# Writing the mask of a windowed attention with four 64x64 products instead of two of 128x128

## The chip, the cores and the metric

One core of a Trainium2 chip runs the whole program. The metric is the device time in microseconds, the median of three runs. The program is written by hand: each engine (TensorE, VectorE, ScalarE, GpSimd and the SyncE DMA queue) has its own list of instructions in a fixed order, and the engines meet only at semaphores.

## What is computed

Two transformer layers, each with a conditioning vector that scales, shifts and gates its two halves. Only the attention of the first layer is touched. For 8 sequences of 512 tokens and width 128, with 16 heads of 64, it is, cut to what matters:

```python
H, D, window_size = (16, 64, 32)
xn = rms_norm(x)
q, k, v = jnp.split(xn @ w_qkv.T, 3, axis=-1)      # 16 heads of 64
q, k = apply_rope(q, cos, sin), apply_rope(k, cos, sin)
attn = jnp.einsum('bhqd,bhkd->bhqk', q, k) * scale
mask = (q_pos >= k_pos) & (q_pos - k_pos <= window_size)
attn = jax.nn.softmax(jnp.where(mask, attn, NEG), axis=-1)
out = jnp.einsum('bhqk,bhkd->bhqd', attn, v)        # then @ w_out.T
```

Each query sees itself and the 32 keys ahead of it. After it follow a router with experts, the second layer's attention and a feed-forward stage in emulated FP4; they stay as they are.

## The kernel before

`phase_attention0` goes through the 8 sequences. A sequence is cut into 16 units: unit `u` has a group of four heads, `q = u // 4`, and a tile of 128 tokens, `t = u % 4`. For a unit the scores are kept for 64 queries at a time: 64 queries see at most 96 keys (the 32 ahead of them and their own 64), so one head gives a block of 64 x 96, and four heads with two halves of the tile fill `psS[:, s]`: 128 partitions (half `a` of the tile on partitions 64a to 64a+63), two PSUM banks (`j`), and in a bank two blocks of 96 columns (`i`).

`score(b, u)` on TensorE fills these banks. First the mask is written: for each bank `j` one bf16 product of a 128x128 identity with 192 columns of the mask table (line 417), which sets the bank to 0 or -1e9. Then the eight fp32 products of queries and keys are added to it (line 425), each of 64x64 weights with 96 columns and thus on one quarter of the array: `j` chooses the rows, `a` the columns. An fp32 product is two instructions. The mask table has two halves of 192 columns: one for `t == 0`, where the first 64 queries of a sequence have no keys ahead of them, and one for the other three tiles.

The order of the work in the body of a unit `u` of sequence `b`:

- TensorE: four transposes of the unit's probabilities into `psT` (line 530), `score(b, u + 2)`, a piece of the projection of the head group after the next (`project`, lines 442 and 447), then, when ScalarE has copied the transposed probabilities, the products with the values into `psO` (line 550), and in units of `t` 2 and 3 a second piece of the projection. After the 16th unit comes the output projection (line 487), after the 8th the transposes of the next sequence's input. `PLAN` gives the pieces: piece 0 in units of t = 0, 1 in t = 1, 2 and 3 in t = 2, 4 and 5 in t = 3.
- VectorE: the division of the probabilities of unit u + 1 (lines 703 and 704), the sine product of one half of a later group (line 676), and the row maxima of unit u + 2 (line 670) together with the sum that ends the rotary embedding (`rope`, line 685). In units of t = 1 this sum stands ahead of the maxima, in the others behind them. `score` of t = 0 waits for this sum. The first units of a sequence also hold steps of the next sequence's normalisation (lines 301, 805 and 808, and line 319 for statistics).
- ScalarE: the copy of the last unit's output (line 626), the copy of the transposed probabilities (line 649, `probT`), the copy of a projected piece out of PSUM (line 589 or 594), the four exponentials of unit u + 2 (line 575).
- GpSimd: one cosine product (line 835, `qk_cos`) for every projected piece of queries or keys, as soon as ScalarE has copied it.
- SyncE: DMAs that swap the halves of a copied piece, and those that lay out the values.

So the score of unit u + 2 is made early: its maxima, exponentials, division and transposes follow in the next two units.

Of the kernel before, what the change touches and what calls it, by code (L numbers as in the profile page):

```python
# [24 lines left out]
HALF = P // 2  # L25
KW = WIN + HALF
# [30 lines left out]
def wait(engine, sem, value):  # L57

    if not (isinstance(value, int) and value <= 0):
        engine.wait_ge(sem, value)  # L60
# [261 lines left out]
def phase_attention0(nc, k):  # L322
# [5 lines left out]
    with ExitStack() as ctx:  # L328
# [13 lines left out]
        psS = ctx.enter_context(nc.psum_tensor("psS", [P, 2, 2, 512], F32))  # L342
# [66 lines left out]
        def _(pe):  # L409
            def score(b, u):  # L410

                q, t = u // TILES, u % TILES
                s, par = u % 2, q % 2
                if t == 0:
                    wait(pe, roped, b * HALVES * QUADS + HALVES * q + HALVES)
                for j in range(2):
                    nc.tensor.matmul(psS[:, s, j, 0:2 * KW], k.ident_bf[:, :], k.mask[:, (t == 0) * 2 * KW:((t == 0) + 1) * 2 * KW],
                                     start=True, stop=False, skip_group_check=True)
                for i in range(2):
                    for a in range(2):  # L420
                        lo = 0 if t == 0 and a == 0 else WIN
                        q0 = t * P + a * HALF
                        for j in range(2):
                            rows = slice(D * j, D * j + D)
                            last = nc.tensor.matmul(psS[a * HALF:(a + 1) * HALF, s, j, i * KW + WIN - lo:(i + 1) * KW],  # L425
                                                    qk[rows, par, i, 0, q0:q0 + HALF],
                                                    qk[rows, par, i, 1, q0 - lo:q0 + HALF],
                                                    start=False, stop=True, skip_group_check=True)
                last.then_inc(scored, 1)
# [54 lines left out]
            def out_project(b, pairs, first, last_):  # L484
# [5 lines left out]
                if last_:  # L490
# [8 lines left out]
                             start=True, stop=True).then_inc(w_turned, 1)  # L499
# [7 lines left out]
            for n in range(len(OPENING)):  # L507
                if OPENING[n] == (0, 1):
                    pe.wait_ge(w_dve, 1)
                if OPENING[n] == (0, 3):  # L510
                    pe.wait_ge(w_act, 2)
                    turn_sixth(4)
                    turn_sixth(5)
                opening(n)
                if OPENING[n] == (1, 1):
                    pe.wait_ge(w_dve, 3)
                    score(0, 0)
                    score(0, 1)
            pe.wait_ge(w_act, 5)

            def body(b, last):
                for u in range(UNITS):
# [9 lines left out]
                    if not (last and u + 2 >= UNITS):  # L532
                        score(b, u + 2)
# [1692 lines left out]
```

## Time and profile before

| | |
|---|---|
| time, median of 3 runs | 1284.41 us (1284.17 to 1285.26) |
| span of the profiled execution | 1295.1 us |
| first attention in it | from about 37 us to 600 us |
| one sequence of it in steady state | 68.6 us |
| PE busy in such a sequence | 62.5 us of 68.6 us |
| mean of a mask product (line 417) | 254 ns, x256 |

The profiled execution has no time of its own beside its span; it is 10.7 us (0.8%) over the median of the timed runs. In the rows, PE is a matmul on TensorE and PEld the load of its weights; a matmul's duration runs from its start to the end of its results, and the next one may start long before that. Rows of the timeline merge instructions of the same line, with their number behind "x".

### The profile page before, as it was taken

To read this page: it belongs to the slowest core of one execution; us is meant where nothing else is said; L and a number is where in the kernel's file an instruction comes from. 1 tells how busy PE (TensorE), PEld (TensorE's weight loads), DVE (VectorE), ACT (ScalarE), POOL (GpSimd) and SP (SyncE) were. 2 spreads that over 40 slices of the span, in tenths; PEclk is the share of its full clock that TensorE was granted. 3 is DMA by queue.
4 is the path that set the end of the run, shared out by engine and by line. 5 is a ranking of instruction groups with operands and counts; after the bars stand their busy time and mean duration, and the time that the engine had idled before them with its cause. 6 is when DMAs were issued, how large, how long until landed. Compare 5 with 4: busy or idle time off the path is not lost. (4 is left out here: it accounts for less than half of the span.)

```text
span 1295.1 us, 25137 instructions
## 1 busy us (share of the span) xinstructions
PE 975.8 (75%) x8604; PEld 662.5 (51%) x8604; DVE 805.3 (62%) x1683; ACT 639.2 (49%) x2132; POOL 430.4 (33%) x332
## 2 busy tenths in 40 slices
PE   6779998989899999985613769747348787867665
PEld 3456565656656565664503556534225454545454
DVE  5777758687777767564657514112136878559995
ACT  3565767767676767671101323112038777643322
POOL 2334333333342423321000857886611312200221
PEclk9789899999999998987555789888759999868967
DMA  6564343434443434431402123445310000000000
GB/s 198 150 182 107 92 123 88 119 96 113 102 113 100 113 83 107 104 91 42 102 0 62 45 59 69 61 73 129 31 66 1 1 2 1 1 1 9 17 17 25
DMA packets 89009, 93.62 MB, mean 72 GB/s; under 512 B 18800, under 2 KB 62304, under 8 KB 88944
## 3 DMA queue, kind: packets, MB, share of 16 engines
q1 hardware_dynamic: 78576, 84.12, 24.7%
q0 software_dynamic: 10368, 8.66, 4.7%
q8 instruction: 37, 0.61, 0.2%
q14 instruction: 28, 0.23, 0.1%
HBM read 24.36 MB, written 10.70 MB: 27 GB/s over the span
## 5 line engine op out<-in xcount | busy, mean ns | idle before, releaser
L835 POOL TENSOR_TENSOR qk_cos<-qk_raw,const 128x512 f32<-128x512 f32 x128 | 183.2, 1432 | 313.0 <-ACT qk_raw L589 313.0
L575 ACT ACTIVATE prob<-psS,neg_max 128x96 f32<-128x96 f32 x512 | 167.9, 342 | 86.5 <-DVE neg_max L670 85.7
L442 PE MATMUL psQ<-a_xnT,weights 128*128 128x512 f32 x250 | 146.0, 668 | 2.1 <-ACT a_xnT L621 1.4
L550 PEld LDWEIGHTS psO<-probT,v_windows 96*64 96x64 f32 x2048 | 73.7, 143 | 142.6 <-ACT probT L649 121.1
L550 PE MATMUL psO<-probT,v_windows 96*64 96x64 f32 x2048 | 91.8, 235 | 43.9 <-ACT probT L649 43.9
L685 DVE TENSOR_TENSOR qk_roped<-qk_cos,qk_swapped 128x512 f32<-128x512 f32 x128 | 119.0, 929 | 5.9 <-DVE qk_swapped L676 5.5
L1508 POOL DMA_INDIRECT sums<-ex_y,ex_index x64 | 97.6, 1525 | 39.5 <-issue 23.5
L1497 POOL DMA_INDIRECT ex_rows<-rows,ex_index x64 | 67.1, 1048 | 121.8 <-DMA ex_index<-lists 102.6
L575 ACT ACTIVATION_READ_ACCUMULATOR prob<-psS,neg_max 128x1 f32 x512 | 105.4, 206 | 0.0
L1442 ACT ACTIVATE ex_hidden<-ex_psH,ex_b 128x512 f32<-128x512 f32 x64 | 43.7, 687 | 114.4 <-PE ex_psH L1401 59.7
L649 ACT COPY probT<-psT 96x512 f32<-96x512 f32 x128 | 76.8, 600 | 46.5 <-PE psT L530 46.5
L589 ACT COPY qk_raw<-psQ 128x512 f32<-128x512 f32 x125 | 74.0, 592 | 48.0 <-PE psQ L442 44.7
L676 DVE TENSOR_TENSOR qk_swapped<-qk_swapped,const 128x512 f32<-128x512 f32 x128 | 88.8, 694 | 14.2 <-DMA qk_swapped<-qk_raw 14.2
L1401 PE MATMUL ex_psH<-ex_hT,ex_w 128*128 128x512 f32 x128 | 69.4, 683 | 18.6 <-ACT ex_hidden L1442 17.8
L530 PE MATMUL psT<-const,prob 128*96 128x128 f32 x512 | 82.3, 285 | 0.0
L703 DVE RECIPROCAL prob_rsum<-prob_sum 128x4 f32<-128x4 f32 x128 | 22.4, 175 | 93.0 <-ACT prob L575 92.9
L704 DVE TENSOR_TENSOR prob<-prob,prob_rsum 128x384 f32<-128x384 f32 x128 | 75.4, 589 | 4.4
L425 PE MATMUL psS<-qk_roped 64*64 64x96 f32 (+1 forms) x2048 | 74.4, 259 | 0.0
L447 PE MATMUL psQ<-weights,a_xnT 128*128 128x256 f32 x252 | 72.7, 412 | 0.0
L670 DVE TENSOR_REDUCE neg_max<-psS 128x4 f32<-128x384 f32 x128 | 70.5, 550 | 3.5 <-PE psS L425 3.5
L1410 PE MATMUL ex_psY<-ex_w,ex_hidden 128*128 128x128 f32 x512 | 64.5, 287 | 10.4 <-issue 10.4
L1410 PEld LDWEIGHTS ex_psY<-ex_w,ex_hidden 128*128 128x128 f32 x512 | 63.1, 203 | 11.6 <-issue 11.5
(317 smaller groups left out, 1936.2 us busy)
## 6 DMA issues: line engine op xcount, KB each, us to landing
qk_swapped<-qk_raw SPq DMA_DIRECT2D x512, 64.0 KB, 2.0
v_windows<-v_tok SPq DMA_DIRECT2D x32, 384.0 KB, 4.4
v_windows<-v_tok SPq DMA_DIRECT2D x32, 256.0 KB, 3.6
mod<-mod_rows SPq DMA_DIRECT2D x12, 512.0 KB, 6.0
ex_w<-in_L_ffn_W SPq DMA_DIRECT2D x16, 256.0 KB
v_windows<-v_tok SPq DMA_DIRECT2D x32, 96.0 KB, 2.1
rows<-rt_h SPq DMA_DIRECT2D x8, 256.0 KB, 2.4
sums<-rt_zeros SPq DMA_DIRECT2D x8, 256.0 KB, 2.7
```

Source lines behind the costliest of these rows:

```text
L425: last = nc.tensor.matmul(psS[a * HALF:(a + 1) * HALF, s, j, i * KW + WIN - lo:(i + 1) * KW], qk[rows, par, i, 0, q0:q0 + HALF], qk[rows, ...
L442: last = nc.tensor.matmul(bank, k.wqkvT[:, col:col + P], xnT[:, :], start=True, stop=True)
L530: ins = nc.tensor.transpose(psT[0:KW, i, :], prob[:, u % 2, i, :], k.ident)
L550: ins = nc.tensor.matmul(psO[D * j:D * j + D, i * P + a * HALF:i * P + (a + 1) * HALF], vw[:, par, a, t, hd], probT[:, 2 * j + i, a * HALF ...
L575: last = nc.scalar.activation(prob[:, s, 2 * j + i, :], psS[:, s, j, i * KW:(i + 1) * KW], ACT.Exp, bias=nmax[:, s, 2 * j + i:2 * j + i + ...
L649: nc.scalar.copy(probT[:, :, :], psT[0:KW, :, :]).then_inc(probT_ready, 1)
L676: return own.mark(nc.vector.tensor_tensor(swp[:, half, :], swp[:, half, :], k.const[:, K_SIN:K_SIN + T], ALU.mult))
L685: nc.vector.tensor_tensor(qk[:, q % 2, half // 2, half % 2, :], rcos[:, half, :], swp[:, half, :], ALU.add).then_inc(roped, 1)
L704: nc.vector.tensor_tensor(prob[:, u % 2, :, :], prob[:, u % 2, :, :], rsum[:, u % 2, :].unsqueeze(2).to_broadcast([P, 4, KW]), ALU.mult).t ...
L835: nc.gpsimd.tensor_tensor(rcos[:, half, :], raw[:, half, :], k.const[:, K_COS:K_COS + T], ALU.mult).then_inc(cos_done, 1)
L1410: last = nc.tensor.matmul(psY[:, n, :], hid[:, d, n // 4, (n % 4) * P:(n % 4 + 1) * P], w2[:, par, d, :], start=(n % 4 == 0 and d == 0), s ...
L1508: nc.gpsimd.indirect_dma_start(k.sums, bass.IndirectOffsetOnAxis(ap=index2[:, par, n:n + 1], axis=0), y[:, par, n, :], None, compute_op=AL ...
```

## The change

In units of t = 1, 2 and 3 the mask is written by four bf16 products of 64x64, one for each quarter of the array, in place of two of 128x128. The product for half `a` and bank `j` takes the 64x64 diagonal block `j` of the identity as weights and rows 64j to 64j+63 of the mask as data; the mask repeats after 64 rows, so that either half serves. Each bank gets the same values as before. Units of t = 0 keep the two full products.

```diff
-                for j in range(2):
-                    nc.tensor.matmul(psS[:, s, j, 0:2 * KW], k.ident_bf[:, :], k.mask[:, (t == 0) * 2 * KW:((t == 0) + 1) * 2 * KW],
-                                     start=True, stop=False, skip_group_check=True)
+                if t == 0:
+                    for j in range(2):
+                        nc.tensor.matmul(psS[:, s, j, 0:2 * KW], k.ident_bf[:, :], k.mask[:, 2 * KW:4 * KW],
+                                         start=True, stop=False, skip_group_check=True)
+                else:
+                    for a in range(2):
+                        for j in range(2):
+                            rows = slice(HALF * j, HALF * (j + 1))
+                            nc.tensor.matmul(psS[a * HALF:(a + 1) * HALF, s, j, 0:2 * KW], k.ident_bf[rows, rows],
+                                             k.mask[rows, 0:2 * KW], start=True, stop=False, skip_group_check=True)
```

## Rows read from the trace of the kernel before

**Rows 1.** The page: span, and busy time of the engines.
```profile
span 1295.1 us, 25137 instructions
PE 975.8 (75%) x8604; PEld 662.5 (51%) x8604; DVE 805.3 (62%) x1683; ACT 639.2 (49%) x2132; POOL 430.4 (33%) x332
```

**Rows 2.** Stretches: us; busy PE, PEld, DVE, ACT, POOL; clock; DMA share; GB/s.
```profile
121.24:193.12 71.88, 65.54 (x742) 43.78 (x741) 51.36 (x97) 48.25 (x193) 26.59 (x20) 0.95 0.40 102
193.12:261.73 68.61, 62.55 (x743) 42.02 (x741) 49.93 (x97) 47.99 (x193) 24.19 (x17) 1.00 0.41 105
```

**Rows 3.** Instructions of the score banks: duration in ns, min/median/max.
```profile
L425 PE MATMUL psS<-qk_roped x2048: 218/243/419, 37.0 to 583.3; 64*64 64x96 f32 x163, 64*64 64x64 f32 x24
L417 PE MATMUL psS<-mask,ident_bf x256: 246/246/368, 36.6 to 582.8; 128*128 128x192 bf16 x128
```

**Rows 4.** Timeline of PE and PEld around a score: start us, us, engine, line.
```profile
251.20 0.33 PE L417 MATMUL psS<-mask,ident_bf 128*128 128x192 bf16 x2
251.45 0.15 PEld L425 LDWEIGHTS psS<-qk_roped 64*64 64x64 f32 x4 [0.16 <-issue]
251.46 0.31 PE L425 MATMUL psS<-qk_roped 64*64 64x96 f32 x4
251.67 0.34 PE L425 MATMUL psS<-qk_roped 64*64 64x96 f32 x8
...
231.85 0.26 PE L417 MATMUL psS<-mask,ident_bf 128*128 128x192 bf16 x1 [0.26 <-DVE qk_roped L685]
```

**Rows 5.** Timeline of units 10 to 13 of a sequence: PE, ACT, DVE.
```profile
233.83 0.60 ACT L649 COPY probT<-psT 96x512 f32<-96x512 f32 x1
234.48 0.69 PE L550 MATMUL psO<-probT,v_windows 96*64 96x64 f32 x16 [0.74 <-ACT probT L649]
...
237.62 0.60 ACT L649 COPY probT<-psT 96x512 f32<-96x512 f32 x1
238.31 0.69 PE L550 MATMUL psO<-probT,v_windows 96*64 96x64 f32 x16
...
242.31 0.59 ACT L589 COPY qk_raw<-psQ 128x512 f32<-128x512 f32 x1 [0.72 <-PE psQ L442]
...
244.24 0.18 DVE L703 RECIPROCAL prob_rsum<-prob_sum 128x4 f32<-128x4 f32 x1 [1.39 <-ACT prob L575]
245.21 0.59 ACT L589 COPY qk_raw<-psQ 128x512 f32<-128x512 f32 x1 [0.28 <-PE psQ L442]
```

**Rows 6.** Timeline of units 4 and 5 of the same sequence.
```profile
210.24 0.59 ACT L589 COPY qk_raw<-psQ 128x512 f32<-128x512 f32 x1 [0.50 <-PE psQ L442]
...
210.90 1.27 POOL L835 TENSOR_TENSOR qk_cos<-qk_raw,const 128x512 f32<-128x512 f32 x1 [2.08 <-ACT qk_raw L589]
211.03 1.69 DVE L685 TENSOR_TENSOR qk_roped<-qk_cos,qk_swapped 128x512 f32<-128x512 f32 x1
...
214.50 0.69 PE L550 MATMUL psO<-probT,v_windows 96*64 96x64 f32 x16 [1.47 <-ACT probT L649]
```

**Rows 7.** Timeline of DVE and POOL: pairs that start within 0.1 us.
```profile
162.16 0.69 DVE L685 TENSOR_TENSOR qk_roped<-qk_cos,qk_swapped 128x512 f32<-128x512 f32 x1 [0.19 <-DVE qk_swapped L676]
162.24 1.75 POOL L835 TENSOR_TENSOR qk_cos<-qk_raw,const 128x512 f32<-128x512 f32 x1 [1.63 <-ACT qk_raw L589]
...
521.61 0.69 DVE L685 TENSOR_TENSOR qk_roped<-qk_cos,qk_swapped 128x512 f32<-128x512 f32 x1 [0.19 <-DVE qk_swapped L676]
521.69 1.75 POOL L835 TENSOR_TENSOR qk_cos<-qk_raw,const 128x512 f32<-128x512 f32 x1 [1.63 <-ACT qk_raw L589]
...
184.91 1.83 POOL L835 TENSOR_TENSOR qk_cos<-qk_raw,const 128x512 f32<-128x512 f32 x1 [2.55 <-ACT qk_raw L589]
184.92 0.68 DVE L685 TENSOR_TENSOR qk_roped<-qk_cos,qk_swapped 128x512 f32<-128x512 f32 x1
...
124.34 1.28 POOL L835 TENSOR_TENSOR qk_cos<-qk_raw,const 128x512 f32<-128x512 f32 x1 [0.41 <-ACT qk_raw L589]
124.40 1.76 DVE L710 TENSOR_TENSOR x<-x,y_mul 128x512 f32 x1
```

## The prediction

> **What bounds the kernel now.** I read the page first: over the whole span TensorE is busy 75% of the time, which says little, because the program is a row of stages [rows 1]. The change lies in the first attention alone, so I cut that out with the view by stretches. In a steady sequence PE is busy 62.55 of 68.61 us at a full clock, VectorE 49.93 and ScalarE 47.99 [rows 2]. So PE is near the bound and has some 6 us of waits per sequence. What a shorter mask is worth depends on where those waits lie: PE time saved ahead of a wait that another engine ends is lost. For that I read the timeline unit by unit.
>
> A score made in unit u belongs to unit u + 2. The changed masks, those of t = 1, 2 and 3, are therefore written in units of t = 3, 0 and 1; those written in units of t = 2 stay. Each kind has a place of its own (units 10 to 13 [rows 5]):
>
> - written in a unit of **t = 1**: in the next unit, of t = 2, PE waits 0.74 us for ScalarE's copy of the probabilities before the value products. That copy hangs on VectorE and ScalarE: exponentials, division, sine product, rope sum, maxima, exponentials. A PE that comes earlier waits longer. Gain: none.
> - written in a unit of **t = 3** (unit 11): the value products start at 238.31, and the copy they need ends at 237.62 + 0.60 = 238.22. In unit 10, where PE does wait, it starts 0.05 behind the copy's end (233.83 + 0.60 = 234.43, start 234.48). PE could start here at 238.27 at the earliest: gain at most 0.04 us.
> - written in a unit of **t = 0** (unit 12): PE runs on without a wait to the projection of piece 0. ScalarE has waited 0.72 us for that piece when it copies it at 242.31, the exponentials stand behind this copy, and VectorE waits 1.39 us for them at 244.24. All of the saving goes on.
>
> So a group of four units gains 0.04 us and one mask's saving.
>
> **The change part by part.** *The mask products.* Two of them take 0.33 us from the first start to the last end and one 0.246, so the second starts 0.08 us behind the first: one pass of 192 columns costs 0.08 [rows 3, 4]. Two full passes are removed. Four products on quarters are added. Four scores start together in the four quarters: the first four are done in 0.31 us where one takes 0.29, and from 251.46 to 251.67 the array takes two rounds of four plus the first load, 0.08 each [rows 3, 4]. If four masks also run abreast, they cost one pass: 0.08 saved.
>
> *The change of tiling.* Between mask and score PE's weight load sits idle 0.16 us [rows 4]: the array empties when it goes from 128x128 to quarters. That moves ahead of the mask, behind the transposes, and is not paid twice: nothing saved, nothing lost. In units with t = 0 scores it stays.
>
> *The first load.* The load behind that gap is not covered: the first four scores take 0.29 us, the median is 0.243, so 0.05 is exposed [rows 3, 4]. Afterwards it is the masks' load that is exposed, and the scores' load goes under the masks. No row shows a bf16 load of 64 columns at full clock. The nearest are the fp32 load of 64 columns, 0.05, and the bf16 load of 128 columns behind a wait, 0.26 against 0.246, so 0.01 [rows 3, 4]. I take half of the fp32 load, 0.03, since an fp32 product is two instructions and a bf16 one is one; the ends are 0.01 and 0.05. The saving of a mask is then 0.08 + 0.05 - 0.03 = 0.10 us, with ends of 0.08 and 0.12.
>
> A page of the Trainium skill, "TensorE: Matmul & The Clock Gate", section "LDWEIGHTS", puts a load at its columns divided by 1.2 GHz, 53 ns for 64 columns of any type outside the fast path. By it the saving is 0.08 and the sum below 2.7 us in place of 3.1; no row here settles it.
>
> *The sum.* A sequence has four groups. Units 11 and 12, and units 15 and the next sequence's 0, are as above. At units 7 and 8 the projection waits for the copy of the next sequence's input, which does not hang on the mask: nothing. At units 3 and 4 the exponentials hang on a busy VectorE, but its rope sum there (211.03) takes 1.69 us because it stands behind GpSimd's cosine product (210.90), which follows ScalarE's copy at 210.24, which has waited 0.50 us for PE [rows 6]. An earlier PE ends the rope sum earlier, and the statistics and the division behind it; I count this group too, with nothing as its other end. Six steady sequences with three groups, two groups in the first, one in the last: 21 x (0.04 + 0.10) = 2.94 us, and some 0.15 in the last units of the last sequence, about one mask: **3.1 us**. The ends: 0.08 and without units 3 and 4, 14 x 0.12 + 0.15 = 1.8; 0.12 and no limit at 0.04, 21 x 0.24 = 5.0. Nothing behind this stage changes: it ends on its output projection, and all later work follows it.
>
> *Instructions and waits.* The change adds two products and two loads in 96 units, no wait, no DMA. Between the waits PE starts scores 0.02 us apart [rows 4], so I cost their issue at nothing.
>
> **Rivals.** *The lock on a shared port.* This is the one I fear. In units of t = 1 the rope sum stands on the path, ahead of the maxima. In 17 such units (sequences 1 to 6) it starts 0.07 to 0.08 us ahead of GpSimd's cosine product and runs in 0.69, while the cosine product is stretched to 1.75 [rows 7]; alone it takes 1.27 [rows 6]. The other way round, where the cosine product started first by 0.13, the rope sum took 1.69 and ended 0.55 behind the cosine product's end (212.17 and 212.72) [rows 6]. So one of the two blocks the other whole. Both come from the same piece 0: the rope sum through exponentials, division and sines, the cosine product through PE's next unit, its mask and its piece 1, whose copy has waited 0.28 us for PE [rows 5]. The mask written in that unit of t = 1, which gains nothing by itself, pulls the cosine product 0.10 us ahead and leaves the rope sum where it is: from 0.08 behind to 0.02 ahead, at the ends from level to 0.05 ahead. The rows at that distance: with GpSimd 0.01 ahead VectorE still ran in 0.68 (184.91, 184.92); with GpSimd 0.06 ahead VectorE took 1.76 (124.34, 124.40) [rows 7]. The turning point is between, and 0.02 lies nearer to the first. If it turns, the rope sum ends 1.27 + 0.55 - 0.02 = 1.80 us after its old start instead of 0.69: 1.1 us, 17 times, on the path. That is 18.7 - 3.1 = 15.6 us slower: **1300.0**.
>
> The skill's "SBUF — State Buffer", section "Who interferes with whom", has the rule: VectorE with two SBUF inputs and GpSimd share a port, and whichever issues first holds it for its whole instruction. Taken by recorded starts it gives this rival at once. The pair at 184.91 does not agree with it at 0.01 us.
>
> *No overlap.* If the four masks went one behind another, they would cost 0.33 instead of 0.16: 0.16 lost at two places of 21 groups, 6.7 us, **1291.1**. The scores' rounds of four speak against it.
>
> *The gain is eaten.* PE waits longer in unit 5, 1.47 us now [rows 6]. In one sequence the granted clock was 0.95 and the sequence took 71.88 us against 68.61 [rows 2]: one more stretch at the lower of its two levels costs 3.3 us and takes the whole gain, **1284.6**. Such a stretch could also go.
>
> *More than that.* If all limits moved along, 5.0 us: **1279.4**.
>
> **How the numbers follow.** The profiled span, 1295.1 us, is 0.8% over the timed median; 3.1 us in it is 1292.0 there, and 1284.4 - 3.1 = **1281.3** timed. The profiler may shift starts by some hundredths, which matters for the lock alone.
>
> Chances: the forecast 0.47, with its own range of 1279.4 to 1282.6; the lock 0.33; no overlap 0.05; eaten 0.11; more 0.04. A measurement tells 0.2%, 2.6 us, from no change. The forecast lies 0.5 us beyond that; I give 0.33 of its 0.47 to faster and 0.14 to same. Faster: 0.33 + 0.04 = 0.37. Same: 0.14 + 0.10 = 0.24. Slower: 0.33 + 0.05 + 0.01 = 0.39. The two signs are nearly even, because the forecast gains little and the lock loses much. The range from 1279.3 to 1302 takes in the lock, since leaving it out would leave more than 2 in 10.
>
> **What would show it.** In the profile after: the scores' 16 instructions start about 0.10 us sooner behind the transposes in units that write a changed mask, and the idle gap is in front of the masks. A steady sequence takes 68.2 us. The rope sum in units of t = 1 still takes 0.69 and starts with the cosine product; if it takes 1.7 to 1.8, the lock has turned and a sequence takes some 71.5. If the sequence stays at 68.6 with earlier scores, the gain lies in PE's waits of units 2, 5 and 6. I am wrong if a mask takes over 0.16 us, or if a step that I hold to be fixed moves along with PE.

## The result and the profile after

The changed kernel takes **1307.34 us** (median of 4 runs, 1306.83 to 1310.32) beside 1284.84 us of the kernel before (4 runs): a ratio of **1.0162 [1.0137, 1.0188]**, so 22.5 us slower. The prediction was 1281.3 us. The first of its rivals, the lock on a shared port, is what happened.

All lines of the changed kernel lie 7 further down (the quarter masks are L424, the full ones L418, the scores L432, the rope sum L692, the cosine product L842). The first lines of the page after:

```profile
span 1305.4 us, 25521 instructions
PE 972.4 (74%) x8796; PEld 651.7 (50%) x8796; DVE 820.8 (63%) x1683; ACT 640.2 (49%) x2132; POOL 419.3 (32%) x332
```

TensorE has 3.4 us less to do than in [rows 1] and VectorE 15.5 us more, with the same 1683 instructions: some of VectorE's instructions have become longer. GpSimd's busy time went down by 11.1 us. That exchange is the lock as one sees it on the first page.

**The masks did what was expected of them.** The timeline of PE and PEld around a score of t = 2, and the group of the quarter masks (durations in ns, min/median/max):

```profile
286.39 0.27 PE L537 MATMUL psT<-const,prob 128*96 128x128 f32 x1
286.60 0.11 PEld L424 LDWEIGHTS psS<-mask,ident_bf 64*64 64x64 bf16 x4 [0.18 <-issue]
286.60 0.28 PE L424 MATMUL psS<-mask,ident_bf 64*64 64x192 bf16 x4
286.70 0.25 PE L432 MATMUL psS<-qk_roped 64*64 64x96 f32 x4
...
L424 PE MATMUL psS<-mask,ident_bf x384: 266/267/367, 38.0 to 604.9; 64*64 64x192 bf16 x192
```

The four masks take 0.28 us together where one takes 0.267, so they run abreast. The gap of the array is now ahead of the masks (0.18) and no longer behind them ([rows 4]: 0.16). The scores begin 0.107 us behind the first mask. From the start of the last transpose to the second round of scores it was 0.50 us before and is 0.39; up to the projection behind the scores it was 0.858 and is 0.739 (medians of the units at full clock in which TensorE waits for nothing in between). So a changed mask saves 0.12 us, which is the upper end of what the sum had; it went by 0.10.

**The rope sum lost its port.** The timeline of GpSimd and VectorE in a unit of t = 1, to be read beside the first and third pair of [rows 7]:

```profile
252.65 1.26 POOL L842 TENSOR_TENSOR qk_cos<-qk_raw,const 128x512 f32<-128x512 f32 x1 [1.51 <-ACT qk_raw L596]
252.69 1.77 DVE L692 TENSOR_TENSOR qk_roped<-qk_cos,qk_swapped 128x512 f32<-128x512 f32 x1 [0.19 <-DVE qk_swapped L683]
```

Before, the cosine product started 0.07 to 0.08 behind the rope sum in all 17 such units, the rope sum ran in 0.69 and the cosine product was stretched to 1.75. After, it starts 0.035 to 0.045 ahead in all 17, runs in its own 1.26, and the rope sum takes 1.77. 17 x 1.08 = 18.4 us. A rope sum in one unit of t = 3 turned as well in most sequences (502.12, 1.77 us), which the prediction had not seen; it turns in `e2_not_t3` below too, and costs nothing there. What now waits longer is seen in the waits of one steady sequence, before (193.12 to 261.73, first fence) and after (342.19 to 414.00): engine, line, what it waited for; us in total, times, longest.

```profile
ACT prob L575 <- DVE neg_max L670: 9.2, 10, 1.3
PEld psS L417 <- DVE qk_roped L685: 1.8, 4, 0.5
```

```profile
ACT prob L582 <- DVE neg_max L677: 12.2, 11, 2.4
PEld psS L418 <- DVE qk_roped L692: 4.9, 3, 1.6
```

Both waits are behind the rope sum: its maxima release the exponentials, and the roped piece releases the scores. Each grew by 3 us in a sequence, three units by 1.1.

**Where the sum ends up.** The six steady sequences take 435.0 us after and 416.3 before, 18.7 more; the first attention ends at 619.33 instead of 599.43, 19.9 later. The views by stretches of two of them (columns as in [rows 2]):

```profile
342.19:414.00 71.81, 62.81 (x766) 41.66 (x765) 52.88 (x97) 48.23 (x193) 22.00 (x17) 0.98 0.39 100
487.18:560.55 73.37, 65.92 (x766) 42.95 (x765) 52.21 (x97) 48.43 (x193) 21.72 (x17) 0.93 0.39 98
...
364.29:365.14 0.85, 0.53 (x12) 0.53 (x14) 0.56 (x2) 0.75 (x2) 0.00 (x0) 0.78 0.62 166
365.14:365.99 0.85, 0.85 (x12) 0.72 (x9) 0.85 (x2) 0.00 (x0) 0.00 (x0) 0.50 0.18 46
```

The last two rows are short pieces of the first: the granted clock falls to its lower level, 1.2 GHz, just after TensorE has waited 1.75 us for a copy of the probabilities (1.47 before, [rows 6]):

```profile
364.61 0.82 PE L557 MATMUL psO<-probT,v_windows 96*64 96x64 f32 x12 [1.75 <-ACT probT L656]
```

In the six sequences 37.5 us lie at that level, against 13.7 before. The 17 longer rope sums less the saving of the masks, about 0.4 us a sequence, would make 18.4 - 2.5 = 15.9 us; the sequences grew by 18.7. By the price that `e2_not_t3` shows below (0.41 us for 3.4 us at the lower level), the 23.9 us more at that level are worth some 2.9: an estimate, but it suggests that the saving was given back there. The profiled spans differ by only 10.3 us, because this profile of before was some 10 us longer behind the first attention than the others (695.6 us, others 683 to 690). Of the 19.9, 1.2 lie outside the six sequences (the work ahead of them is 4.3 longer, the last sequence 3.1 shorter). The timed 22.5 is 2.6 more than the 19.9 of the profile; that remainder was not traced.

### The profile page after: what moved, and what is told of

The parts are those of the page before. It is cut to its first block and busy times, and to the rows that moved or that the text cites. A ratio compares the mean times of both kernels' runs of the same rounds, so it can differ in the third digit from the quotient of the medians.

```text
span 1305.4 us, 25521 instructions
## 1 busy us (share of the span) xinstructions
PE 972.4 (74%) x8796; PEld 651.7 (50%) x8796; DVE 820.8 (63%) x1683; ACT 640.2 (49%) x2132; POOL 419.3 (32%) x332
## 5 line engine op out<-in xcount | busy, mean ns | idle before, releaser
L842 POOL TENSOR_TENSOR qk_cos<-qk_raw,const 128x512 f32<-128x512 f32 x128 | 171.6, 1341 | 345.7 <-ACT qk_raw L596 345.6
L449 PE MATMUL psQ<-a_xnT,weights 128*128 128x512 f32 x250 | 150.8, 688 | 5.9 <-ACT a_xnT L628 3.9
L692 DVE TENSOR_TENSOR qk_roped<-qk_cos,qk_swapped 128x512 f32<-128x512 f32 x128 | 143.5, 1121 | 5.9 <-DVE qk_swapped L683 5.5
L454 PE MATMUL psQ<-weights,a_xnT 128*128 128x256 f32 x252 | 75.4, 425 | 0.0
L432 PE MATMUL psS<-qk_roped 64*64 64x96 f32 (+1 forms) x2048 | 70.1, 254 | 0.0
L1884 DVE TENSOR_REDUCE a_nmax<-a_psS 128x1 f32<-128x512 f32 x64 | 41.1, 683 | 36.6 <-PE a_psS L1683 36.4
```

Source lines behind the costliest of these rows:

```text
L449: last = nc.tensor.matmul(bank, k.wqkvT[:, col:col + P], xnT[:, :], start=True, stop=True)
L454: last = nc.tensor.matmul(bank[:, i * 4 * D:(i + 1) * 4 * D], xnT[:, t * P:(t + 1) * P], k.wqkvT[:, col:col + 4 * D], start=(i == 0), stop ...
L692: nc.vector.tensor_tensor(qk[:, q % 2, half // 2, half % 2, :], rcos[:, half, :], swp[:, half, :], ALU.add).then_inc(roped, 1)
L842: nc.gpsimd.tensor_tensor(rcos[:, half, :], raw[:, half, :], k.const[:, K_COS:K_COS + T], ALU.mult).then_inc(cos_done, 1)
```

## The experiments

The theory: the quarter mask of t = 3, which gains nothing, pulls the cosine product ahead of the rope sum, and the port costs 1.1 us at 17 places; the masks of t = 1 and 2 gain what the sum says. The rivals: the cost lies in another of the three masks, in the quarters as such or in the lower clock, or the long rope sum is a sign of a delay and not its cause.

### One kind of mask at a time

`e2_not_t3` keeps the full masks for t = 3; the other two kinds are in quarters. The line that chooses is shown; in this and the other three runs of this kind the full mask again takes the half of the table that belongs to its `t`, as in the kernel before (not shown).

```diff
-                if t == 0:
+                if t in (0, 3):
```

> The changed kernel, but with the two full masks again for the scores of t = 3, which are written in units of t = 1. Quarter masks stay for t = 1 and 2. Lock theory: only the t = 3 mask pulls the cosine product ahead of the rope sum, so the rope sum starts 0.08 us first again and takes 0.69; all of the gain stays: a steady sequence of 68.2 us, 1281 to 1283 us. Clock rival and mask rival: a third of the change is undone, so a third of the loss goes: about 1300 us.

It took 1286.90 us beside 1287.67: 1.0007 [0.9987, 1.0028]. The loss is gone, though the expected 1281 to 1283 us are not reached. The rope sum is 0.075 us ahead again and takes 0.69. A pair, and two neighbouring sequences:

```profile
365.87 0.69 DVE L692 TENSOR_TENSOR qk_roped<-qk_cos,qk_swapped 128x512 f32<-128x512 f32 x1 [0.19 <-DVE qk_swapped L683]
365.95 1.74 POOL L842 TENSOR_TENSOR qk_cos<-qk_raw,const 128x512 f32<-128x512 f32 x1 [1.63 <-ACT qk_raw L596]
...
259.47:328.08 68.61, 63.09 (x758) 42.11 (x757) 50.12 (x97) 48.22 (x193) 23.46 (x17) 0.98 0.41 105
328.08:396.28 68.20, 61.76 (x758) 40.98 (x757) 49.77 (x97) 48.01 (x193) 23.95 (x17) 1.00 0.42 106
```

At a full clock a sequence takes 68.20, the forecast to the hundredth. Three of the six have 3.4 us at the lower clock; two of these take 68.61 and 68.62, what the kernel before takes at a full clock (the first sequence takes 70.33). In the timed median the gain of 3 us is not to be seen, and the interval, which ends 1.7 us below the kernel before, does not reach it.

`e3_only_t3` is the other half: only the mask of t = 3 in quarters.

```diff
-                if t == 0:
+                if t != 3:
```

> The kernel before, but with quarter masks for the scores of t = 3 alone. Lock theory: the whole loss and none of the gain: the rope sum takes about 1.77 us in units of t = 1, a steady sequence takes 71.8 to 72 us, the time is 1303 us (17 times 1.1 more than before) or up to the 1307 of the changed kernel. Clock rival and mask rival: a third of the loss, about 1292 us.

1308.74 us beside 1287.67, 1.0163 [1.0135, 1.0192]: the whole loss of the change, from one of its three masks. A pair, and a sequence at full clock:

```profile
308.54 1.26 POOL L842 TENSOR_TENSOR qk_cos<-qk_raw,const 128x512 f32<-128x512 f32 x1 [1.51 <-ACT qk_raw L596]
308.59 1.76 DVE L692 TENSOR_TENSOR qk_roped<-qk_cos,qk_swapped 128x512 f32<-128x512 f32 x1 [0.19 <-DVE qk_swapped L683]
...
269.54:341.36 71.82, 62.27 (x751) 41.50 (x749) 52.72 (x97) 48.00 (x193) 22.75 (x17) 1.00 0.40 100
```

68.61 [rows 2] + 3 x 1.07 = 71.82. The clock has no part in this sequence.

`e9_only_t2` and `e10_only_t1` change one of the other two alone (`if t != 2:` and `if t != 1:` in the same place).

> The kernel before, but with quarter masks for the scores of t = 2 alone, which are written in units of t = 0. By the sum of the prediction each of three groups per steady sequence gains a whole mask's saving, 0.10 us: 68.3 us for a sequence at full clock, against 68.60 before. The rope sums of t = 1 stay at 0.69. Rival (PE's waits swallow these masks too): 68.6.

> The kernel before, but with quarter masks for the scores of t = 1 alone, which are written in units of t = 3. By the sum of the prediction the copy of the transposed probabilities ends 0.04 us ahead of PE's need there, so each of three groups per steady sequence gains 0.04 us only: 68.48 us for a sequence at full clock. If it gained the whole saving: 68.3. If nothing: 68.60.

One run each: 1286.37 and 1287.07 us beside a single 1280.87 of before. Single runs of before went from 1280.87 to 1296.11 in these studies, so the times say nothing; the sequences at full clock do. First only t = 2, then only t = 1:

```profile
331.61:399.95 68.34, 62.07 (x751) 41.48 (x750) 49.83 (x97) 47.99 (x193) 24.21 (x17) 1.00 0.41 106
```

```profile
333.26:401.72 68.46, 62.28 (x750) 41.50 (x749) 49.91 (x97) 48.02 (x193) 23.93 (x17) 1.00 0.41 105
```

68.61 - 68.34 = 0.27, forecast 3 x 0.10; 68.61 - 68.46 = 0.15, forecast 3 x 0.04. Together 0.42, and 68.61 - 68.20 = 0.41 in the run with both.

The 0.27 is not three equal parts, though. The transposes and the projection of unit 12 and, in unit 0, the projection with what it waits for; first before, then with only t = 2 in quarters (the transposes of unit 0 start with the sequence, at 193.12 and 331.61):

```profile
193.46 0.69 DVE L824 TENSOR_TENSOR y_mul<-psQ,mod 128x512 f32<-128x512 f32 x1 [6.21 <-PE psQ L487]
194.31 1.12 PE L442 MATMUL psQ<-a_xnT,weights 128*128 128x512 f32 x2
...
239.89 0.60 PE L530 MATMUL psT<-const,prob 128*96 128x128 f32 x4
241.08 1.12 PE L442 MATMUL psQ<-a_xnT,weights 128*128 128x512 f32 x2
```

```profile
331.94 0.69 DVE L831 TENSOR_TENSOR y_mul<-psQ,mod 128x512 f32<-128x512 f32 x1 [6.19 <-PE psQ L494]
332.78 1.12 PE L449 MATMUL psQ<-a_xnT,weights 128*128 128x512 f32 x2
...
378.23 0.60 PE L537 MATMUL psT<-const,prob 128*96 128x128 f32 x4
379.30 1.12 PE L449 MATMUL psQ<-a_xnT,weights 128*128 128x512 f32 x2
```

In unit 12 the projection starts 1.19 us behind the transposes before and 1.07 after: the whole 0.12 goes on. In unit 0 it is 1.19 and 1.17. There the program makes the projection wait until VectorE has read the last output projection out of the same bank (`y_mul`, which ends some 0.15 us ahead of it both times), so that only 0.02 is left. By the starts of the units, the masks of t = 2 gain 0.02 in unit 0, 0.13 in unit 4, nothing in unit 8 and 0.12 in unit 12; those of t = 1 gain 0.04 to 0.05 in each of three places.

### The same mask, made longer

If the order at the port is the cause, the fast mask must become harmless when it is given more work. The masks of t = 3 stay in quarters, and write 48, 96 or 144 columns more, into columns of the bank that nothing reads. 192 columns cost 0.08 us [rows 3, 4], so the cosine product should come later by 0.02, 0.04 and 0.06. The run with 96 came first; the other two were forecast from it. Lines lie one further down than in the changed kernel.

```diff
-                            nc.tensor.matmul(psS[a * HALF:(a + 1) * HALF, s, j, 0:2 * KW], k.ident_bf[rows, rows],
-                                             k.mask[rows, 0:2 * KW], start=True, stop=False, skip_group_check=True)
+                            wide = 2 * KW + (96 if t == 3 else 0)     # e7_pad48: 48, e8_pad144: 144
+                            nc.tensor.matmul(psS[a * HALF:(a + 1) * HALF, s, j, 0:wide], k.ident_bf[rows, rows],
+                                             k.mask[rows, 0:wide], start=True, stop=False, skip_group_check=True)
```

> The changed kernel with the masks of t = 3 48 columns wider (240), 0.02 us more of TensorE in units of t = 1. The cosine product is then 0.02 us ahead of the rope sum in units 1, 9 and 13. In the run with 96 columns the rope sum won at 0.004 and lost at 0.009 to 0.011. Lock theory: all three lose, rope sums of 1.78 us, a steady sequence of 71.5 to 71.9, about 1307 us.

> The changed kernel, but the four masks of t = 3 are 288 columns wide instead of 192: the 96 more go to columns of the bank that nothing reads. TensorE works 96 columns longer per unit of t = 1, which is 0.04 us. Lock theory: that puts the cosine product from 0.04 us ahead of the rope sum to about level with it, which is on VectorE's side of the turning point (VectorE won with GpSimd 0.01 ahead): the rope sum is back at 0.69 us, and a kernel that works more is 24 us faster than the changed one: 1281 to 1284 us. Clock rival: 1306 us. Mask rival: a little over 1307 us.

> The changed kernel with the masks of t = 3 144 columns wider (336), 0.06 us more of TensorE in units of t = 1 than in the changed kernel. The rope sum then starts 0.01 to 0.02 us ahead of the cosine product. Lock theory: all 17 rope sums take 0.69 us; a steady sequence of 68.2 us, 1282 to 1287 us, 20 us faster than the changed kernel with less mask work. If loss came from TensorE's own time, it would be over 1307 us.

| columns more | time, us | ratio | GpSimd ahead of the rope sum, ns | rope sums of 17 that take 1.8 us |
|---|---|---|---|---|
| 0 (the change) | 1307.34 | 1.0162 [1.0137, 1.0188] | +35 to +45 | 17 |
| 48 | 1308.42 (one run) | | +16 to +29 | 17 |
| 96 | 1294.92 | 1.0064 [1.0033, 1.0095] | 0 to +11 | 5, each the first unit of t = 1 in its sequence |
| 144 | 1282.64 | 0.9968 [0.9948, 0.9987] | -10 to -20 | none |

With 48 columns a rope sum loses at a lead of GpSimd of 0.016 to 0.029 us. A pair:

```profile
307.43 1.26 POOL L843 TENSOR_TENSOR qk_cos<-qk_raw,const 128x512 f32<-128x512 f32 x1 [1.53 <-ACT qk_raw L597]
307.44 1.79 DVE L693 TENSOR_TENSOR qk_roped<-qk_cos,qk_swapped 128x512 f32<-128x512 f32 x1 [0.19 <-DVE qk_swapped L684]
```

The one with 96 columns lies on the edge, and both ways occur in one run; the expected 1281 to 1284 us were missed. Two pairs of it, in the first unit of t = 1 of a sequence and in a later one:

```profile
198.19 1.26 POOL L843 TENSOR_TENSOR qk_cos<-qk_raw,const 128x512 f32<-128x512 f32 x1 [1.46 <-ACT qk_raw L597]
198.20 1.80 DVE L693 TENSOR_TENSOR qk_roped<-qk_cos,qk_swapped 128x512 f32<-128x512 f32 x1 [0.19 <-DVE qk_swapped L684]
...
231.68 1.82 POOL L843 TENSOR_TENSOR qk_cos<-qk_raw,const 128x512 f32<-128x512 f32 x1 [1.55 <-ACT qk_raw L597]
231.69 0.69 DVE L693 TENSOR_TENSOR qk_roped<-qk_cos,qk_swapped 128x512 f32<-128x512 f32 x1 [0.19 <-DVE qk_swapped L684]
```

The rows round to hundredths; in nanoseconds GpSimd is 9 to 11 ahead where the rope sum loses and 0 to 5 where it wins. With 144 columns the rope sum is ahead everywhere:

```profile
379.12 0.69 DVE L693 TENSOR_TENSOR qk_roped<-qk_cos,qk_swapped 128x512 f32<-128x512 f32 x1 [0.19 <-DVE qk_swapped L684]
...
379.14 1.80 POOL L843 TENSOR_TENSOR qk_cos<-qk_raw,const 128x512 f32<-128x512 f32 x1 [1.58 <-ACT qk_raw L597]
...
189.79:258.12 68.33, 62.97 (x766) 41.30 (x765) 50.10 (x97) 48.35 (x193) 23.57 (x17) 0.98 0.42 108
```

This kernel gives TensorE more to do than the changed one and is 25 us faster. That shows the order at the port as the cause; a delay elsewhere, with the long rope sum as its sign, would not go away when more work is added.

### The order fixed by a wait

The other way is to leave the masks alone and let GpSimd wait for the rope sum before its cosine product. `e1_cos_waits`, ahead of the cosine product:

```diff
+                    q6, half6 = ahead(u, 6)
+                    if u % TILES == 1 and not (last and q6 >= QUADS):
+                        wait(pool, roped, b * HALVES * QUADS + HALVES * q6 + half6 + 1)
```

> The changed kernel, but in units of t = 1 GpSimd waits for that unit's rope sum before its cosine product. Lock theory (in the changed kernel the cosine product starts 0.04 us ahead of the rope sum and holds it up by 1.1 us, 17 times): the rope sum is back at 0.69 us, a steady sequence takes 68.2 us instead of 71.8, and the time is 1281 to 1283 us. Clock rival (shorter masks leave TensorE idle for longer, its granted clock falls more often, and that is the loss): nothing of it is undone, 1307 us. Mask rival (quarter masks cost TensorE more than full ones): 1307 us.

1296.71 us, 1.008 [1.0054, 1.0106]: half the loss gone, and the expectation missed. All rope sums of t = 1 run in 0.69, yet a sequence takes 70.70:

```profile
263.50:334.20 70.70, 61.62 (x766) 40.41 (x765) 52.75 (x97) 47.99 (x193) 23.96 (x17) 1.00 0.40 102
...
273.27 1.27 POOL L842 TENSOR_TENSOR qk_cos<-qk_raw,const 128x512 f32<-128x512 f32 x1 [0.54 <-ACT qk_raw L596]
...
273.46 1.50 DVE L711 TENSOR_TENSOR prob<-prob,prob_rsum 128x384 f32<-128x384 f32 x1
...
289.71 3.00 POOL L842 TENSOR_TENSOR qk_cos<-qk_raw,const 128x512 f32<-128x512 f32 x2
289.82 1.76 DVE L683 TENSOR_TENSOR qk_swapped<-qk_swapped,const 128x512 f32<-128x512 f32 x1
```

The wait stood one product too early. GpSimd runs ahead of VectorE by a piece, and the product that collides is the one that it issues in its own unit of t = 2. The wait in t = 1 held back that product and the one before it, and these now meet VectorE's division (1.50 us, 0.56 where nothing meets it) and its sine product (1.76, else 0.69). The lock was not removed but moved to other work.

`e5_cos_waits_right` puts the wait at the product that collides, and `e6_cos_waits_all` at every one.

```diff
+                    q5, half5 = ahead(u, 5)
+                    if u % TILES == 2 and not (last and q5 >= QUADS):    # e6: without u % TILES == 2
+                        wait(pool, roped, b * HALVES * QUADS + HALVES * q5 + half5 + 1)
```

> The changed kernel, but in units of t = 2 GpSimd waits, before its cosine product, for the rope sum of the unit ahead (t = 1). In the first try the wait stood one cosine product too early: the product that collides with the rope sum of a unit of t = 1 is the one that GpSimd issues in its unit of t = 2, because the copy that it needs comes ahead of time. Lock theory: the rope sum takes 0.69 us again, the cosine product starts some 0.8 us later than it would and runs in 1.27, and nothing waits for it: a steady sequence of 68.2 us, 1282 to 1286 us (as with full masks for t = 3). If a sequence stays at 70.7 us as in the first try, the wait itself costs something that I do not see.

> The changed kernel, but GpSimd waits before every cosine product for the rope sum of the unit ahead, so that no rope sum on VectorE is ever held up. In the kernel before, the rope sum of the units 2 and 4 took 1.32 and 1.69 us, units 6 and 10 likewise. Lock theory: rope sums of 0.69 us everywhere, so the VectorE chain of units 2 to 6 gets shorter by 0.6 to 1.6 us per sequence on top of 68.2: 66.6 to 67.6 us, 1272 to 1280 us. Rival: the cosine products come so late that the rope sum of the next unit waits for them: 69 us or more, 1288 us.

1284.29 us, 0.9971 [0.9949, 0.9992], and 1283.40 us, 0.9972 [0.9954, 0.999], both beside 1286.83. First a sequence of the one, then of the other with the wait that is longest in total:

```profile
327.50:396.00 68.50, 61.60 (x767) 40.42 (x766) 50.05 (x97) 48.03 (x193) 22.74 (x17) 1.00 0.41 105
```

```profile
330.10:398.76 68.66, 61.50 (x767) 40.51 (x766) 48.67 (x97) 48.11 (x193) 22.08 (x17) 1.00 0.41 105
...
POOL qk_cos L842 <- DVE qk_roped L692: 32.6, 13, 3.4
```

With the order fixed, the full change no longer loses. 68.50 is 0.30 over the 68.20 of `e2_not_t3`: the wait is not free. The four normalisation steps (line 301) of unit 1, first in `e2_not_t3`, then in `e5_cos_waits_right` with the cosine product that was held back:

```profile
335.05 1.60 DVE L301 TENSOR_SCALAR a_h<-x,mean,rstd 128x128 f32 x4
```

```profile
334.25 1.27 POOL L842 TENSOR_TENSOR qk_cos<-qk_raw,const 128x512 f32<-128x512 f32 x1 [2.33 <-DVE qk_roped L692]
334.47 1.90 DVE L301 TENSOR_SCALAR a_h<-x,mean,rstd 128x128 f32 x4
```

They start 6.97 us into the sequence in both and take 0.30 longer beside the later product, in five of the six steady sequences; the maxima of unit 2 stand 0.26 later. For `e6_cos_waits_all` I had expected a sequence below 67.6, since every rope sum of a steady sequence then runs in 0.69; it takes 68.66. VectorE is busy 1.4 us less than in `e5_cos_waits_right` and nothing comes of it: the rope sums of the other units were not what bounds those units. What does there was not settled.

## Why the prediction was wrong

**The sum held, in part by luck.** The sequence with the masks of t = 1 and 2 takes the predicted 68.20. A mask of t = 1 gains 0.04 to 0.05 in three groups (predicted 0.04), and one of t = 3 nothing (`e3_only_t3` has no sign of a gain in its 71.82). The masks of t = 2 were to gain 3 x 0.10 and gain 0.02 + 0.13 + 0.12. Two misses offset each other there: a mask saves 0.12 and not 0.10, and in unit 0, which the sum held to be like unit 12, the projection stands behind a wait for VectorE that the kernel shows and the prediction passed over. The masks run abreast, so the rival "no overlap" is out. On the exposed load, the estimate by the section "LDWEIGHTS" of the Trainium skill's "TensorE: Matmul & The Clock Gate" was 0.08 for a mask; the trace shows 0.12, so the measurement decides for the smaller load.

**The step that failed is the turning point of the lock.** The prediction named this mechanism, its place, its 17 units and its price of 1.1 us (measured 1.08), and left it at 0.33 with the words "The turning point is between, and 0.02 lies nearer to the first". Two things were wrong in it.

- The *turning point*. It was bracketed by the pairs 0.01 and 0.06 [rows 7], and the lower one was taken as the nearer. For a rope sum that waits 0.19 us behind its sine product, it lies between 0.005 and 0.009 us. At 0.02 it turns as well: `e7_pad48` stands at 0.016 to 0.029, and all 17 lost. The pair at 184.91 was no measure for that: its rope sum stands in a queue behind a maximum, and such rope sums have a turning point of their own. They won at 0.012 to 0.021 in `e1_cos_waits` and at up to 0.024 in the other runs, and lost from 0.029 on (473.41 in the changed kernel). Why the two kinds differ in recorded starts is open. The row of the same form and the same releaser was the one to look for, and the trace of before had none near zero.
- The *pull*. The cosine product came 0.115 earlier, not 0.10, in line with the 0.12 that a mask saves, which put it 0.035 to 0.045 ahead and not 0.02. By itself this decided nothing.

The rule of the Trainium skill's "SBUF — State Buffer", section "Who interferes with whom", that whichever of the two issues first holds the port, was set against the pair at 184.91 in the prediction. For this rope sum it holds to within 0.01 us of the recorded starts (the table above), so it was the better guide of the two.

**The rival's own time was too low.** It was 1300.0, the medians differ by 22.5 and not by 15.6. The price of the lock was right, but the 3.1 us were not there to be taken off: by the estimate above they went into the lower clock, as in the rival "the gain is eaten", which came on top of the lock and was not weighed together with it. That makes 18.7; the other 3.8 us of the timed difference stay open. Why the changed kernel spends more time at 1.2 GHz is not shown either. The longer waits alone do not explain it: in its profile `e3_only_t3` has the same long rope sums, and its six sequences lie 13.7 us at that level, no more than before. It also stays open why the medians of `e5_cos_waits_right` and `e6_cos_waits_all` (like that of `e8_pad144` near 0.997) show a gain, though their sequences at full clock gain 0.11 us and nothing, and that of `e2_not_t3`, whose sequence gains 0.41, does not; its interval touches theirs.

## What to carry to other kernels

When an instruction off the critical path becomes shorter, look at what it releases and at which pairs on a shared resource then start in another order: set the margin between their starts (here 0.075 us) against the shift (0.115). If the shift is larger, count the change of order as the likely case, at the price of the longer instruction, and not as a side risk. The mask that gained nothing should have stayed as it was; where an order must be kept, the wait belongs at the very product that collides, since one product earlier it moves the collision elsewhere. And before a saving is counted in one place because it counts in another, look in the kernel for a wait that only the one has, as unit 0 had here.

## What the runs showed of the hardware

For a rope sum that waits 0.19 us behind its sine product, the order at the shared port turns where GpSimd's recorded start is between 5 and 9 ns ahead; for one that stands in VectorE's queue, between 24 and 29 ns. When both start together, the one that loses takes longer by 1.1 us if it is VectorE's and by 0.5 if it is GpSimd's, at 512 elements a partition each. Thus 96 columns of useless work in the masks of t = 3 made the time 12 us shorter, and 144 columns 25. That adding work to TensorE makes a kernel faster by 2% I had not expected.
